# Mamba scan on one core: the product for the state behind the block products, its sum behind y

## The chip, the cores and the metric

The kernel runs on one NeuronCore of one Trainium2 chip. The metric is the device time of one execution in microseconds, lower is better. It is given as the median of several runs.

## The reference

One block of a model: half a feed-forward layer, a Mamba-2 mixer (the "attention" of the names), and half a feed-forward layer again, each behind a layer norm, for 2048 tokens of 256 channels in float32. What the change touches is the mixer's recurrence:

```python
dt = jax.nn.softplus(dt + dt_bias)
A = -jnp.exp(A_log)
dA = jnp.exp(dt * A).reshape(b, l, G, HPG)
dtx = dt.reshape(b, l, G, HPG)[..., None] * x

def step(state, inp):
    dA_t, dtx_t, B_t, C_t = inp
    state = state * dA_t[..., None, None] + jnp.einsum('bgcp,bgn->bgcpn', dtx_t, B_t)
    y_t = jnp.einsum('bgn,bgcpn->bgcp', C_t, state)
    return (state, y_t)
...
y = jnp.moveaxis(ys, 0, 1) + D.reshape(1, 1, G, HPG, 1) * x
...
yn = (yg * lax.rsqrt(var + EPS)).reshape(b, l, INTER) * norm_w
out = yn * jax.nn.silu(z)
return out @ out_proj_w
```

There are 64 heads of 8 channels (512 inner channels) and a state of 128 numbers for each channel.

## The kernel before

The program has three stages that follow each other: the first feed-forward layer (it also builds the weights from a lookup table), the input projection with the convolution, and build_scan, which holds the recurrence, the out projection and the second feed-forward layer. The change is in build_scan, which takes 244 to about 430 us of the span for the recurrence.

**How the scan is tiled.** The 2048 tokens are 16 tiles of 128, and a tile is 4 blocks (NB) of 32 tokens (Q). The recurrence is done blockwise. For a tile, y has three parts: "intra", what the tokens of a block give each other (the block products, L855); "prior", what earlier blocks of the same tile give (L942, from w); and what the state before the tile gives (XB, L935). The state after the tile is the decayed old state (tmp, L1215) plus the product "new" (L947) of B with the fourth of GpSimd's weighted inputs w (L1198); VectorE adds the two (L1151).

**How it is staged.** steps() yields 18 steps c. In step c tile a = c is prepared (transposes, decays, masks), tile b_ = c - 1 gets its products and its state, and tile z = c - 2 gets the gate, its variance and the out projection. Each engine has its own program, written out by hand in the order in which it runs, and engines meet at semaphores: wait(engine, name, value) is left out where the value is zero. There is no scheduler: the order on an engine is the order of the source.

**The decays** of a tile come in 5 units that alternate between two PSUM banks (seg): TensorE sums the logs (segments, L840 for unit 0 and L845 for units 1 to 4), ScalarE takes the exponent in place (L991, for unit 0 into "ends", L995), VectorE multiplies by gs into mmat (masked, L1067). Unit n may be written by TensorE once unit n - 2 was read by VectorE ("m_ok").

**TensorE's order in a step** is: transposes of x (L906), of B and its products (L909 to L913), unit 0, transposes of y of tile z (L922), units 1 and 2, XB from the state (L935), prior (L942), new (L947), unit 3, half of the block products (L855), the out projection (L964, L967) and the row sum (L969), the other half of the block products, unit 4.

**VectorE's order** is: xdt (L1092), yf, u and the two sums of squares (L1100 to L1116), masks 1 and 2, y from XB (L1137), prior times its decay (L1141), their sum (L1146), the state's sum (L1151), mask 3, the residual of tile z (L1157), y plus intra (L1162), mask 4.

**GpSimd's order** is: gs (L1210), tmp (L1215), the low part of u (L1221), w of blocks 0 and 1 (L1198), rstd (L1232), w of blocks 2 and 3. The w of blocks 0 to 2 wait for "prior" of the tile before, the w of block 3 waits for "new":

```python
wait(pool, "prior_ok" if n < NB - 1 else "new_ok", a)
```

The last tile needs no state after it, so it has no "new". ScalarE's copy of BG into bg (L1013) also waits for "new_ok", of the tile before the last one.

Of the kernel before, what the change touches and what calls it, by code (L numbers as in the profile page):

```python
# [23 lines left out]
ALU = mybir.AluOpType  # L24
ACT = mybir.ActivationFunctionType

P = 128
# [21 lines left out]
NB = P // Q  # L49
# [704 lines left out]
def build_scan(nc, T, norm, out):  # L754
# [3 lines left out]
    with ExitStack() as ctx:  # L758
# [10 lines left out]
        w = T["w"]  # L769
        ends = [sb(f"ends_{b}", [P, EW]) for b in range(2)]  # L770
        xdt = [sb(f"xdt_{b}", [P, INTER]) for b in range(2)]
        state = [sb(f"state_{b}", [P, INTER]) for b in range(2)]
        bg = [sb(f"bg_{b}", [P, 2 * P + Q]) for b in range(2)]
        gs = [sb(f"gs_{b}", [P, Q]) for b in range(2)]
        tmp, y, yf, sq, u = (sb(n, [P, INTER]) for n in ("tmp", "y", "yf", "sq", "u"))
# [10 lines left out]
        s = {n: sem("c_" + n) for n in names}  # L786
# [7 lines left out]
        LAST = TILES - 1  # L794
# [3 lines left out]
        def wait(eng, name, value):  # L798
            if value > 0:
                eng.wait_ge(s[name], value)  # L800
# [28 lines left out]
        def _(pe):  # L829
# [72 lines left out]
            for a, b_, z, do_a, do_b, do_z in steps():  # L902
# [27 lines left out]
                if do_b:  # L930
                    wait(pe, "xdt_ok", min(a, TILES - 1) + 1)
                    wait(pe, "state_ok", b_ + 1)
                    for b in range(NB):
                        for g in range(4):
                            ins = pe.matmul(XB[Q * g:Q * g + Q, P * b:P * b + P], cv[:, b_, 5, Q * b:Q * b + Q],  # L935
                                            state[b_ % 2][:, P * g:P * g + P], start=True, stop=True)
                    ins.then_inc(s["from_ok"], 1)
                    wait(pe, "w_ok", NB * (b_ + 1) if b_ < LAST else NB * LAST + NB - 1)
                    wait(pe, "y1_ok", b_)
                    for b in range(1, NB):  # L940
                        for g in range(4):
                            ins = pe.matmul(prior[Q * g:Q * g + Q, P * b:P * b + P],  # L942
                                            bg[b_ % 2][:, P + Q * b:P + Q * b + Q], w[:, b - 1, P * g:P * g + P],
                                            start=True, stop=True)
                    ins.then_inc(s["prior_ok"], 1)
                    if b_ < LAST:
                        pe.matmul(new[:, :], bg[b_ % 2][:, 0:P], w[:, NB - 1, :], start=True, stop=True  # L947
                                  ).then_inc(s["new_ok"], 1)
                    else:
                        wait(pe, "m_ok", (UNITS - 1) * TILES)  # L950
                        norm.pe_transpose(pe, 0)
                if do_a:
# [19 lines left out]
                    hidden(0, 0)  # L972
                if do_b:
                    block_products(b_, HG // 2, HG).then_inc(s["intra_ok"], 1)
                if do_a:
                    segments(a, 4)
            for g in range(GROUPS):
# [83 lines left out]
        def _(dve):  # L1061
# [25 lines left out]
            for a, b_, z, do_a, do_b, do_z in steps():  # L1087
# [56 lines left out]
                if do_b:  # L1144
                    wait(dve, "t1_ok", b_ + 1)
                    dve.tensor_tensor(y[:, P:], prior[:, P:], y[:, P:], ALU.add).then_inc(s["y1_ok"], 1)  # L1146
                if do_b and b_ < LAST:
                    wait(dve, "new_ok", b_ + 1)
                    wait(dve, "tmp_ok", b_ + 1)
                    wait(dve, "from_ok", b_)  # L1150
                    dve.tensor_tensor(state[(b_ + 1) % 2][:, :], new[:, :], tmp[:, :], ALU.add).then_inc(s["state_ok"], 1)  # L1151
                if do_a:
                    masked(a, 3)
                if do_z:
# [4 lines left out]
                if do_b:  # L1159
                    wait(dve, "intra_ok", b_ + 1)  # L1160
                    wait(dve, "y1_ok", b_ + 1)
                    dve.tensor_tensor(y[:, :], intra[:, :, :, :].rearrange("p b h d -> p (b h d)"), y[:, :], ALU.add  # L1162
                                      ).then_inc(s["y_ok"], 1)
                if do_a:
                    masked(a, 4)
                if a == LAST - 1:
# [166 lines left out]
```

## Time and profile before

| | us |
|---|---|
| median of 3 runs | 528.63 |
| lowest and highest run | 528.18 and 531.5 |
| the profiled execution | 529.64 |
| its span | 527.9 |
| TensorE busy in the span | 473.7 (90%) |
| TensorE's weight loads | 396.9 (75%) |
| VectorE busy | 373.4 (71%) |
| ScalarE busy | 285.5 (54%) |
| GpSimd busy | 160.8 (30%) |

The span is what the trace covers, and some 1.7 us of the execution's time lie outside it. In the rows, PE is TensorE's matmuls, PEld its weight loads, DVE is VectorE, ACT is ScalarE and POOL is GpSimd. A matmul that multiplies in float32 stands as two records, so "x64" in the trace is 32 matmuls. The end of a matmul is modelled, so two records that follow each other can overlap by a tenth. A row of the windows view gives the stretch, its length, the busy time of PE, PEld, DVE, ACT and POOL with the number of instructions, the granted TensorE clock as a share of 2.4 GHz, the mean busy share of the DMA engines and the rate. "Issue" is time in which an engine waited for nothing that the trace shows.

### The profile page before, as it was taken

The numbers are of one execution on the slowest core, as the hardware profiler recorded it, in microseconds if no ns is written. First come the engines' busy times: TensorE is split into PE (matmuls) and PEld (weight loads), VectorE is DVE, ScalarE is ACT, GpSimd is POOL, SyncE is SP. The second block draws the span as 40 slices with busy tenths as digits, with TensorE's granted clock in tenths as the row PEclk, the third lists the DMA queues.
The fourth block names the chain that finished last, engine by engine and source line by source line (L and its number), as shares of the span: only waits on it lengthen the run. The fifth ranks groups of instructions, "written<-read, shape, count | busy, mean of one in ns | idle before, by whom it ended". The sixth has DMA issues, their size and how long they took to land.

```text
span 527.9 us, 17119 instructions
## 1 busy us (share of the span) xinstructions
PE 473.7 (90%) x7478; PEld 396.9 (75%) x7478; DVE 373.4 (71%) x736; ACT 285.5 (54%) x515; POOL 160.8 (30%) x216
## 2 busy tenths in 40 slices
PE   4999999999989889366899999999968899999996
PEld 3658797988878668355778877888666778898986
DVE  6998836465659996942688888888758966565543
ACT  3658525252447769796576666566645533233241
POOL 1100040203141221004567766676646411000000
PEclk9999999999999989688899999999999999999999
DMA  8950070000000000010000000000170000101011
GB/s 205 237 197 1 1 338 1 1 1 1 0 1 0 2 0 1 0 40 22 4 6 4 5 4 6 6 4 4 50 297 4 3 3 0 41 1 40 1 40 41
DMA packets 7163, 21.31 MB, mean 40 GB/s; under 512 B 688, under 2 KB 5296, under 8 KB 6448
## 3 DMA queue, kind: packets, MB, share of 16 engines
q1 hardware_dynamic: 6688, 18.05, 10.2%
q10 hardware_dynamic: 400, 2.16, 1.8%
q8 instruction: 59, 0.97, 0.7%
q14 instruction: 16, 0.13, 0.1%
HBM read 12.87 MB, written 6.55 MB: 37 GB/s over the span
## 4 chain that ended last, share of the span: by engine, by line
PE 39%; issue 5%; DVE 3%; ACT 3%; POOL 3%; POOLq 0%; DVEq 0%; ACTq 0%
PE intra L855 6%; PE seg L845 3%; PE yo L964 3%; PE XB L935 2%; PE new L947 1%; PE XB L906 1%; PE seg L840 1%; POOL w L1198 1%; PE yo L922 1%; PE yo L967 1%; PE prior L942 1%; ACT seg L991 1%; DVE mmat L1067 1%; PE XB L68 1%; PE BG L68 1%
## 5 line engine op out<-in xcount | busy, mean ns | idle before, releaser
L1198 POOL TENSOR_TENSOR w<-xdt,ends 32x512 f32<-32x512 f32 (+3 forms) x63 | 66.5, 1074 | 3.1 <-PE prior L942 3.1
L614 DVE SCALAR_TENSOR_TENSOR cv<-pre,vec,cv 128x512 f32<-128x512 f32 x72 | 53.2, 750 | 8.0 <-ACT cv L657 6.3
L991 ACT ACTIVATE seg<-seg 128x512 f32<-128x512 f32 x64 | 36.0, 578 | 32.8 <-PE seg L845 32.5
L1067 DVE TENSOR_TENSOR mmat<-seg,gs 128x512 f32<-128x512 f32 x64 | 42.4, 684 | 10.3 <-ACT seg L991 10.2
L506 POOL TENSOR_TENSOR n_rstd<-n_ve,m_half 128x4 f32<-128x4 f32 x12 | 13.8, 1146 | 115.7 <-DVE n_ve L502 115.7
L845 PEld LDWEIGHTS seg<-abk,m_seg 96*32 96x32 bf16 x2048 | 20.6, 96 | 27.2 <-DVE mmat L1067 14.4
L845 PE MATMUL seg<-abk,m_seg 96*32 96x64 bf16 x2048 | 27.3, 195 | 10.8 <-issue 7.3
L1004 ACT ACTIVATE f_hT<-f_h 128x512 fp32r<-128x512 f32 (+1 forms) x24 | 15.2, 632 | 40.1 <-DVE f_h L1078 40.1
L68 PE MATMUL pj<-n_xT,win 128*128 128x512 f32 x88 | 35.6, 405 | 1.1 <-PEq L130 1.1
L70 PE MATMUL pj<-n_xT,win 128*128 128x512 f32 x88 | 34.8, 395 | 0.0
L69 PE MATMUL pj<-n_xT,win 128*128 128x512 f32 x88 | 34.7, 395 | 0.0
L371 ACT ACTIVATE f_hT<-f_h 128x512 fp32r<-128x512 f32 (+1 forms) x24 | 15.2, 633 | 34.6 <-DVE f_h L295 34.5
L1221 POOL TENSOR_TENSOR uh<-u,uh 128x512 fp32r<-128x512 f32 x16 | 21.0, 1313 | 40.5 <-ACT uh L1025 37.9
L1082 DVE TENSOR_TENSOR f_hT<-f_h,f_hT 128x512 fp32r<-128x512 f32 (+1 forms) x24 | 16.6, 691 | 16.8 <-ACT f_hT L1004 16.8
L299 DVE TENSOR_TENSOR f_hT<-f_h,f_hT 128x512 fp32r<-128x512 f32 (+1 forms) x24 | 16.6, 690 | 14.0 <-ACT f_hT L371 14.0
L255 DVE TENSOR_SCALAR mask_d<-gu_idx,entry 128x1408 fp32r<-128x1408 int32 x28 | 24.4, 947 | 2.3 <-DMA gu_idx<-in_gu 2.3
L367 ACT ACTIVATE f_sg<-f_gate 128x512 f32<-128x512 f32 (+1 forms) x24 | 14.1, 587 | 19.2 <-PE f_gate L70 19.0
L68 PE MATMUL f_down<-wd,f_hT 128*128 128x256 f32 x80 | 22.9, 286 | 0.3 <-ACT wd L344 0.3
L69 PE MATMUL f_down<-wd,f_hT 128*128 128x256 f32 x80 | 22.5, 281 | 0.0
L70 PE MATMUL f_down<-wd,f_hT 128*128 128x256 f32 x80 | 22.5, 281 | 0.0
L295 DVE TENSOR_TENSOR f_h<-f_sg,f_up 128x512 f32<-128x512 f32 x20 | 13.7, 685 | 10.7 <-PE f_up L70 7.4
L68 PEld LDWEIGHTS pj<-n_xT,win 128*128 128x128 f32 x88 | 17.1, 194 | 4.6 <-issue 1.2
(244 smaller groups left out, 1455.2 us busy)
## 6 DMA issues: line engine op xcount, KB each, us to landing
wgu_dram<-wgu SPq DMA_DIRECT2D x1, 2816.0 KB, 8.2
wgu<-wgu_dram SPq DMA_DIRECT2D x1, 2816.0 KB, 10.4
out<-x_res SPq DMA_DIRECT2D x4, 512.0 KB, 2.9
x_res<-in_x SPq DMA_DIRECT2D x1, 1536.0 KB, 23.8
wd_dram<-wd SPq DMA_DIRECT2D x1, 1536.0 KB, 11.6
wd<-wd_dram SPq DMA_DIRECT2D x1, 1536.0 KB, 13.7
gu_idx<-in_gu ACTq DMA_DIRECT2D x4, 352.0 KB, 7.9
gu_idx<-in_gu SPq DMA_DIRECT2D x4, 352.0 KB, 12.5
```

The lines of the kernel that those rows point to most:

```text
L68: pe.matmul(out, w_hi, x_hi, start=start, stop=False)
L69: pe.matmul(out, w_hi, x_lo, start=False, stop=False)
L70: return pe.matmul(out, w_lo, x_hi, start=False, stop=stop)
L255: dve.tensor_scalar(dst, src, entry[:, p:p + 1], None, ALU.is_equal).then_inc(mask_ok, 1)
L299: dve.tensor_tensor(low_part(hT, c, r), h[0:r, :], hT[0:r, 0, c, :].bitcast(F32), ALU.subtract).then_inc(h_lo, 1)
L614: dve.scalar_tensor_tensor(dst, pre[:, x, k:k + GN].rearrange("p (t c) -> p t c", c=P), cw[:, x, k:k + 1], dst, ALU.mult, ALU.add).then_in ...
L845: ins = pe.matmul(out[Q * b:Q * b + Q, i, :], T["m_seg"][:, IU * (n - 1) + i, :], T["abk"][:, b, a, :], start=True, stop=True)
L855: ins = pe.matmul(intra[Q * g:Q * g + Q, :, hh, :], mmat[b_ % 2][:, :, h], xbd[b_ % 2][:, h, :, :], start=True, stop=True)
L991: act.activation(seg[u_ % 2][:, :, :], seg[u_ % 2][:, :, :], ACT.Exp).then_inc(s["exp_ok"], 1)
L1067: dve.tensor_tensor(mmat[a % 2][:, i, :], seg[u_ % 2][:, :, :], gs[a % 2][:, i].unsqueeze(2).broadcast_to([P, IU, HEADS]), ALU.mult).then_ ...
L1198: pool.tensor_tensor(heads(w[r, n, :]), heads(xdt[a % 2][r, :]), ends[a % 2][r, n * HEADS:(n + 1) * HEADS].unsqueeze(2) .broadcast_to([Q * ...
L1221: pool.tensor_tensor(uh[:, 1, :, :].rearrange("p g t -> p (g t)"), u[:, :], uh[:, 0, :, :].bitcast(F32).rearrange("p g t -> p (g t)"), ALU ...
```

## The change

TensorE issues "new" no longer behind prior but behind the second half of the block products, ahead of unit 4; there it waits for all four w of the tile. At the old place the wait for w is one less, since prior reads only three of them. VectorE adds the state no longer behind the sum of y and prior but behind the sum of y and intra, ahead of mask 4. The waits of GpSimd and ScalarE read as before.

```diff
--- before.py
+++ after.py
@@ -935,7 +935,7 @@
                             ins = pe.matmul(XB[Q * g:Q * g + Q, P * b:P * b + P], cv[:, b_, 5, Q * b:Q * b + Q],
                                             state[b_ % 2][:, P * g:P * g + P], start=True, stop=True)
                     ins.then_inc(s["from_ok"], 1)
-                    wait(pe, "w_ok", NB * (b_ + 1) if b_ < LAST else NB * LAST + NB - 1)
+                    wait(pe, "w_ok", NB * b_ + NB - 1)
                     wait(pe, "y1_ok", b_)
                     for b in range(1, NB):
                         for g in range(4):
@@ -943,10 +943,7 @@
                                             bg[b_ % 2][:, P + Q * b:P + Q * b + Q], w[:, b - 1, P * g:P * g + P],
                                             start=True, stop=True)
                     ins.then_inc(s["prior_ok"], 1)
-                    if b_ < LAST:
-                        pe.matmul(new[:, :], bg[b_ % 2][:, 0:P], w[:, NB - 1, :], start=True, stop=True
-                                  ).then_inc(s["new_ok"], 1)
-                    else:
+                    if b_ == LAST:
                         wait(pe, "m_ok", (UNITS - 1) * TILES)
                         norm.pe_transpose(pe, 0)
                 if do_a:
@@ -972,6 +969,11 @@
                     hidden(0, 0)
                 if do_b:
                     block_products(b_, HG // 2, HG).then_inc(s["intra_ok"], 1)
+                if do_b and b_ < LAST:
+                    wait(pe, "w_ok", NB * (b_ + 1))
+                    wait(pe, "state_ok", b_ + 1)
+                    pe.matmul(new[:, :], bg[b_ % 2][:, 0:P], w[:, NB - 1, :], start=True, stop=True
+                              ).then_inc(s["new_ok"], 1)
                 if do_a:
                     segments(a, 4)
             for g in range(GROUPS):
@@ -1144,11 +1146,6 @@
                 if do_b:
                     wait(dve, "t1_ok", b_ + 1)
                     dve.tensor_tensor(y[:, P:], prior[:, P:], y[:, P:], ALU.add).then_inc(s["y1_ok"], 1)
-                if do_b and b_ < LAST:
-                    wait(dve, "new_ok", b_ + 1)
-                    wait(dve, "tmp_ok", b_ + 1)
-                    wait(dve, "from_ok", b_)
-                    dve.tensor_tensor(state[(b_ + 1) % 2][:, :], new[:, :], tmp[:, :], ALU.add).then_inc(s["state_ok"], 1)
                 if do_a:
                     masked(a, 3)
                 if do_z:
@@ -1161,6 +1158,11 @@
                     wait(dve, "y1_ok", b_ + 1)
                     dve.tensor_tensor(y[:, :], intra[:, :, :, :].rearrange("p b h d -> p (b h d)"), y[:, :], ALU.add
                                       ).then_inc(s["y_ok"], 1)
+                if do_b and b_ < LAST:
+                    wait(dve, "new_ok", b_ + 1)
+                    wait(dve, "tmp_ok", b_ + 1)
+                    wait(dve, "from_ok", b_)
+                    dve.tensor_tensor(state[(b_ + 1) % 2][:, :], new[:, :], tmp[:, :], ALU.add).then_inc(s["state_ok"], 1)
                 if do_a:
                     masked(a, 4)
                 if a == LAST - 1:
```

**TensorE, one step in the middle of the scan.** A row is a line of the source, its operation, the tile that it writes, the tiles that it reads, and its shape. Before:

```order
L942 MATMUL prior<-w,bg 32x128 x12
L947 MATMUL new<-w,bg 128x512
L845 MATMUL seg<-abk,m_seg 32x64 x32
L855 MATMUL intra<-xbd_even,mmat 32x4x8 x32
L964 MATMUL yo<-wout,uh 128x256 x8
L967 MATMUL yo<-wout,uh 128x256 x4
L969 MATMUL yo<-ones,ssum 128x1
L855 MATMUL intra<-xbd_even,mmat 32x4x8 x32
L845 MATMUL seg<-abk,m_seg 32x64 x32
L906 MATMUL XB<-ident,cv 128x128 x4
```

After (the lines from L947 on have moved up by three, so that L961, L964 and L966 are L964, L967 and L969 of before):

```order
L942 MATMUL prior<-w,bg 32x128 x12
L845 MATMUL seg<-abk,m_seg 32x64 x32
L855 MATMUL intra<-xbd_even,mmat 32x4x8 x32
L961 MATMUL yo<-wout,uh 128x256 x8
L964 MATMUL yo<-wout,uh 128x256 x4
L966 MATMUL yo<-ones,ssum 128x1
L855 MATMUL intra<-xbd_even,mmat 32x4x8 x32
L975 MATMUL new<-w,bg 128x512
L845 MATMUL seg<-abk,m_seg 32x64 x32
L906 MATMUL XB<-ident,cv 128x128 x4
```

The product "new" has moved behind unit 3, both halves of the block products and the out projection, and stands directly in front of unit 4, behind which the next step's transposes begin.

**VectorE, the same stretch,** from the masks of units 1 and 2 to the next step's xdt. Before:

```order
L1067 TENSOR_TENSOR mmat<-seg,gs 128x512 x2
L1137 TENSOR_TENSOR y<-XB,dl 128x512
L1141 TENSOR_TENSOR prior<-prior,dl 128x384
L1146 TENSOR_TENSOR y<-prior,y 128x384
L1151 TENSOR_TENSOR state<-new,tmp 128x512
L1067 TENSOR_TENSOR mmat<-seg,gs 128x512
L1157 SCALAR_TENSOR_TENSOR x_res<-yo,rstd_y,x_res 128x256
L1162 TENSOR_TENSOR y<-intra,y 128x512
L1067 TENSOR_TENSOR mmat<-seg,gs 128x512
L1092 TENSOR_TENSOR xdt<-XB,dt_tok 128x512
L1100 SCALAR_TENSOR_TENSOR yf<-cv,vec,yo 128x128 x4
```

After (lines are two further down, L1165 is the state's sum):

```order
L1069 TENSOR_TENSOR mmat<-seg,gs 128x512 x2
L1139 TENSOR_TENSOR y<-XB,dl 128x512
L1143 TENSOR_TENSOR prior<-prior,dl 128x384
L1148 TENSOR_TENSOR y<-prior,y 128x384
L1069 TENSOR_TENSOR mmat<-seg,gs 128x512
L1154 SCALAR_TENSOR_TENSOR x_res<-yo,rstd_y,x_res 128x256
L1159 TENSOR_TENSOR y<-intra,y 128x512
L1165 TENSOR_TENSOR state<-new,tmp 128x512
L1069 TENSOR_TENSOR mmat<-seg,gs 128x512
L1094 TENSOR_TENSOR xdt<-XB,dt_tok 128x512
L1102 SCALAR_TENSOR_TENSOR yf<-cv,vec,yo 128x128 x4
```

The sum of the state has moved behind mask 3, the residual and the sum of y, and stands in front of mask 4 and of the next step's xdt.

## Rows read from the trace of the kernel before

**Rows 1.** Waits of the scan, 244 to 415 us: total us, times, longest us

```profile
PEld seg L845 <- DVE mmat L1067: 14.4, 16, 1.6
```

**Rows 2.** Timeline, one step: start us, us, engine line op out<-in xcount [idle before <-releaser]

```profile
343.97 2.11 POOL L1198 TENSOR_TENSOR w<-xdt,ends 96x512 f32<-96x512 f32 x2
...
344.36 0.66 PE L906 MATMUL XB<-ident,cv 128*128 128x128 f32 x4
...
345.13 0.69 DVE L1067 TENSOR_TENSOR mmat<-seg,gs 128x512 f32<-128x512 f32 x1
...
345.62 0.41 ACT L1013 ACTIVATE bg<-BG 128x288 f32<-128x288 f32 x1 [0.52 <-PE BG L913]
...
346.60 1.12 DVE L1100 SCALAR_TENSOR_TENSOR yf<-cv,vec,yo 128x128 f32<-128x128 f32 x4 [0.18 <-PE yo L922]
...
348.87 1.12 PE L947 MATMUL new<-w,bg 128*128 128x512 f32 x2
...
349.30 1.28 DVE L1067 TENSOR_TENSOR mmat<-seg,gs 128x512 f32<-128x512 f32 x2
...
350.04 0.42 PE L845 MATMUL seg<-abk,m_seg 96*32 96x64 bf16 x32
...
350.28 1.15 PE L855 MATMUL intra<-xbd,mmat 128*32 128x32 f32 x64
...
351.36 1.22 PE L964 MATMUL yo<-wout,uh 128*128 128x256 f32 x8
...
352.16 0.68 DVE L1151 TENSOR_TENSOR state<-new,tmp 128x512 f32<-128x512 f32 x1
...
353.09 1.14 PE L855 MATMUL intra<-xbd,mmat 128*32 128x32 f32 x64
...
354.04 0.46 PE L845 MATMUL seg<-abk,m_seg 96*32 96x64 bf16 x32
...
354.43 0.66 PE L906 MATMUL XB<-ident,cv 128*128 128x128 f32 x4
```

**Rows 3.** Timeline, the same place in two other steps

```profile
328.01 1.13 PE L947 MATMUL new<-w,bg 128*128 128x512 f32 x2
...
328.24 1.28 DVE L1067 TENSOR_TENSOR mmat<-seg,gs 128x512 f32<-128x512 f32 x2
...
329.06 0.42 PE L845 MATMUL seg<-abk,m_seg 96*32 96x64 bf16 x32
...
382.11 1.28 DVE L1067 TENSOR_TENSOR mmat<-seg,gs 128x512 f32<-128x512 f32 x2
...
382.85 0.42 PE L845 MATMUL seg<-abk,m_seg 96*32 96x64 bf16 x32
```

**Rows 4.** Windows, 12 steps (length, busy times, PEclk, DMA share, GB/s), and timeline, one hole

```profile
271.02:402.38 131.36, 122.77 (x4352) 102.89 (x4345) 107.01 (x218) 80.77 (x156) 88.01 (x97) 1.00 0.10 39
...
390.54 0.41 PE L845 MATMUL seg<-abk,m_seg 96*32 96x64 bf16 x31 [2.63 <-issue]
```

**Rows 5.** Timeline, step 15 and the start of step 16

```profile
410.07 0.42 PE L845 MATMUL seg<-abk,m_seg 96*32 96x64 bf16 x32 [0.74 <-DVE mmat L1067]
...
415.35 0.66 PE L922 MATMUL yo<-ident,y 128*128 128x128 f32 x4 [0.82 <-DVE y L1162]
```

**Rows 6.** Windows: four stretches of the scan, columns as in rows 4

```profile
245.00:255.00 10.00, 6.95 (x284) 5.74 (x280) 5.15 (x8) 9.03 (x17) 5.79 (x8) 0.88 0.01 3
...
344.36:354.43 10.07, 10.02 (x369) 8.36 (x363) 8.86 (x19) 6.70 (x13) 7.31 (x9) 1.00 0.02 5
384.00:392.00 8.00, 5.19 (x174) 4.80 (x174) 3.66 (x7) 1.71 (x4) 4.01 (x5) 1.00 0.98 419
406.00:412.00 6.00, 4.72 (x159) 3.66 (x160) 5.90 (x13) 3.85 (x8) 4.71 (x6) 1.00 0.01 4
```

**Rows 7.** DMA queues of the page: packets, MB, share of 16 engines

```profile
q8 instruction: 59, 0.97, 0.7%
```

**Rows 8.** Line L935: duration ns min/median/max, first and last start us

```profile
L935 PE MATMUL XB<-state,cv x512: 269/273/421, 252.2 to 416.7; 128*32 128x128 f32 x171
```


## The prediction

> **What bounds the kernel now.** I read the waits over the scan first, then one step of it in the timeline, then the same place in two other steps, then the busy times over 12 steps, and last the stretches that are not like the others.
>
> The waits show that TensorE is the engine the scan waits on, with one regular exception: the segment matmuls wait for VectorE's masks, 14.4 us in 16 times on the weight loads [rows 1]. In that view no TensorE line waits for GpSimd's w (L1198): the wait on "w_ok" that the change loosens costs nothing today.
>
> One step tells where the exception sits [rows 2]. I count from its first transpose, L906 at 344.36; the next is at 354.43, so a step is 10.07 us. The segment matmul of unit 3 starts at 350.04, 5.68 us in. The first half up to there is a chain: transposes of y, then yf on VectorE at 346.60 (which waited 0.18 for them), the square on ScalarE, the sums and the first mask at 349.30. One mask takes 0.69 (345.13), so it ends at 349.99, and TensorE goes on 0.05 us after it. TensorE's own work there (up to prior) ends near 348.87, where "new" starts. So "new" lies in a hole of about 1.1 us that TensorE has anyway. The second half, 350.04 to 354.43, is 4.39 us of TensorE work end to end: segments, half of the block products, the out projection (L964), the other half at 353.09, segments at 354.04, transposes.
>
> Does "new" or the mask open unit 3? In two other steps [rows 3] the mask ends at 382.11 + 0.69 = 382.80 with segments at 382.85 (0.05 behind it, as above), and at 328.24 + 0.69 = 328.93 with segments at 329.06. Only the second is later than 0.05, by 0.08; there "new", started at 328.01, is what ended last, and it held TensorE 1.05 us. So mask and "new" end together almost to a tenth: the matmul fills the hole exactly.
>
> Twelve steps in a row, from the L906 at 271.02 to that at 402.38, take 131.36 us [rows 4]; 12 times 10.07 is 120.84. The other 10.5 us are holes that the trace calls "issue"; the longest, 2.63 us, stands in front of segments at 390.54 [rows 4].
>
> **The change part by part.**
>
> *The matmul leaves the first half.* TensorE then waits for the mask from the end of prior on. The chain over yf, square and mask has no step that waits for "new", so its 5.68 us stay. Gain: the excess of 0.08 us in a few steps, 0.2 us in all. Bounds: 0, or 14 times 1.05 if the mask were not the gate.
>
> *It comes back behind the second half of the block products.* No hole is there, so it is paid in full. Its body is 1.05 us [rows 3]. Its edges cost too: from the first of a half's block products to what follows takes 350.28 to 351.36, 1.08 us, where a full-width matmul follows, and 353.09 to 354.04, 0.95 us, where segments follow [rows 2]. So 0.13 more for changing to a 128-row matmul, 1.18 us a step. From below I bound it by 1.05, if the edge costs nothing, from above by 1.12 (its modelled length at 348.87) plus twice the edge, 1.38. I take 1.18, since the rows for body and edge are its own.
>
> There are 15 such products, 14 of them in steps that have an out projection. In the first one (step 1) TensorE has no hole at the old place, so the move costs only the edge, 0.13. Thirteen steps pay 1.18: 15.3 us. The fifteenth (step 15, where unit 3 waits 0.74 us for the mask because VectorE first takes the layer-norm statistics) is followed by y's transposes that wait 0.82 us for VectorE [rows 5]. That wait hides part of the matmul, but the state's sum (0.68 us) now stands before mask 4 and the normalisation, which TensorE's next transposes need. I count 1.0, bounds 0.3 and 1.3.
>
> *VectorE: the sum moves behind y, before mask 4.* It waits for "new", which ends where the segments of unit 4 begin, 0.39 us before the next step (354.04 against 354.43). So it runs from about -0.33 to +0.35 of the next step. Behind it stand mask 4, xdt and yf. Mask 4 starts at +0.77 (345.13) because ScalarE's exponent of unit 4 comes only then; that is what hides the sum, with 0.4 us to spare. y itself ends before, as its block products end 1.4 us before the step. Cost nothing; 0.68 a step if that cover is gone. Mask 3 comes 0.68 earlier, which nobody waits for.
>
> *The waits on w and state.* "prior" now needs three of the four w instead of four: worth nothing [rows 1]. GpSimd's fourth w (one of two in 2.11 us, 343.97) now waits for "new" of the same step: it runs from -0.39 to +0.68. Queued behind it is gs, which cannot start before ScalarE's copy of BG (345.62 + 0.41, that is +1.67), then tmp. So it has 1.0 us of room; without it, masks would be late by up to 1.07 a step. The state is there at +0.35 and wanted later: by tmp, which stands behind gs, and by XB, which stands behind y's transposes (yf starts on their end, 346.60, at +2.24). No DMA is issued or passed.
>
> *Issue holes.* They total 10.5 us. The same instructions now run in steps 1.1 us longer, and TensorE waits 1.1 us near the middle, in which whatever feeds it can catch up; a hole ahead of yf still lengthens the chain. Bounds: all 10.5 gone, or 2 more through another alignment. I take 2.0 off, because the largest ones stand at 384 to 392, where transfers are 98% busy [rows 6], and will stay.
>
> Sum: 15.3 + 1.0 + 0.1 - 0.2 - 2.0 = 14.2 us. The profiled execution took 529.64 us (span 527.9, 1.7 around it), so 543.8. The median of the runs shown is 528.63, 1.0 less; I predict 543.0.
>
> **Rivals.**
>
> *The loading of TensorE's code paces the holes* (chance 0.11). There are 59 loads of 0.97 MB together, 16.4 KB each [rows 7]. The Trainium skill, page "Advanced Engine Details and Errata", section "ISA Cache", says that instructions come in blocks of 16 KB, 256 instructions; the rows agree. If the added wait cures all 10.5 us: 16.2 - 10.5 = +5.7, 534.3. For it: holes sit in front of the densest instruction runs. Against: the step of [rows 2] has 10.02 us busy in 10.07 at the same density [rows 6], and the longest hole comes with the transfers.
>
> *"new" was the gate* (0.06): then 1.05 leaves the first half and only the edges stay, 14 x 0.13 = 1.8, minus the holes: 529. For it: in all three steps read the segments begin about when "new" ends. Against: segments 0.05 us behind the mask in two of the three steps read.
>
> *Faster: code loading is the bound of the whole scan* (0.03). Then the matmul's time at its new place, in front of the segments where the 2.63 hole stands, is spent loading, and the holes go as well: 528.6 - 10.5 = 518. It decides from where a step without holes would still take longer than its matmuls. Against: the same row, TensorE 10.02 us busy in 10.07 [rows 6].
>
> *VectorE or GpSimd late into the next step* (0.06): if the state's sum does not fit in front of mask 4, 14 x 0.68 = 9.5 more, 552.
>
> *TensorE's clock falls* (0.04). It stood at 0.88 in 245 to 255 with TensorE 6.95 of 10 us busy, so part of that was at 1.2 GHz, and at 1.00 in 406 to 412 with 4.72 of 6 busy; a new step has 10.0 of 11.2 busy [rows 6]. An XB matmul takes 421 ns at most against 273 in the median [rows 8]. One step in four at that ratio: 3.5 x 10 x 0.54 = 19 us more on top of the forecast, 562. The Trainium skill, page "TensorE: Matmul & The Clock Gate", section "A second HAM failure mode: psum-queue depth-cycling", says that frequent short pauses between groups of matmuls make the clock swing between its levels. By that rule a pause in every step is bad; the row of 406 to 412, with pauses of 0.7 and more, does not bear it out.
>
> **How the numbers follow.** The forecast has 0.70. Its own range is 538 to 547 (price 1.05 to 1.38 a step, holes by -5 to +2, not all at their ends together); the range of 8 in 10 reaches down to the code-loading case: 535 to 547. A measurement of this kernel tells about 1% from no change, that is 523.3 to 533.9. Faster by over 1%: 0.03. Within 1%: 0.06 of "new was the gate" and 0.04 of the low edge of the code-loading case, 0.10. Slower: 0.87.
>
> **What would show it.** In the profile after, a step without holes lasts 11.25 us; its unit-3 segments start 5.7 us in and wait about 1.1 us for the mask, so the waits of segments for masks go from 14.4 to about 28 us on the weight loads; "new" stands between the block products and the segments, 1.2 us from the one to the other; mask 4 still starts 0.8 us into the step, and gs at 1.7. I am wrong if the first half shrinks to about 4.6 us, if yf starts behind xdt instead of the transposes, or if issue holes in the scan fall by more than 5 us.

## The result and the profile after

The changed kernel takes 539.61 us (median of 4 runs, 538.27 to 541.06) against 530.03 us of the kernel before (median of 4, 528.18 to 531.5): ratio 1.0183, 95% interval 1.0132 to 1.0235. It is slower, by 9.6 us. The profiled execution took 541.06 us, the slowest of the four, against 529.64 us before: 11.4 us more in the two traces.

The page of the changed kernel begins:

```profile
span 539.3 us, 17134 instructions
...
PE 473.0 (88%) x7478; PEld 395.9 (73%) x7478; DVE 375.4 (70%) x736; ACT 285.0 (53%) x515; POOL 161.2 (30%) x216
...
PEclk9999999999999989679999999999979999999999
...
q8 instruction: 59, 0.97, 0.7%
```

The busy times are those of before to 2 us; what is new is idle time of TensorE. The waits of the changed kernel from 244 to 430 us (total us, times, longest us) say in front of what:

```profile
PEld seg L845 <- DVE mmat L1069: 22.4, 16, 2.1
...
PE seg L845 <- DVE mmat L1069: 18.4, 16, 1.8
...
POOL w L1200 <- PE new L975: 10.6, 14, 5.1
...
DVE state L1165 <- PE new L975: 2.0, 3, 1.3
```

The first line answers to [rows 1]: the weight loads waited 14.4 us for masks before. The matmul line of before was:

```profile
PE seg L845 <- DVE mmat L1067: 2.8, 8, 0.9
```

So TensorE itself now waits 15.6 us more for masks, 1.1 us in each of 14 steps. GpSimd's fourth w waits for "new", as its place in the new order says.

One step of the changed kernel in the timeline, which answers to [rows 2]:

```profile
338.69 0.69 DVE L1165 TENSOR_TENSOR state<-new,tmp 128x512 f32<-128x512 f32 x1
...
338.83 1.08 POOL L1200 TENSOR_TENSOR w<-xdt,ends 128x512 f32<-128x512 f32 x1 [0.33 <-PE new L975]
...
338.93 0.66 PE L906 MATMUL XB<-ident,cv 128*128 128x128 f32 x4
...
339.70 0.69 DVE L1069 TENSOR_TENSOR mmat<-seg,gs 128x512 f32<-128x512 f32 x1 [0.31 <-ACT seg L993]
...
340.67 0.25 POOL L1212 TENSOR_TENSOR gs<-bg,tri 128x32 f32<-128x32 f32 x1 [0.77 <-ACT bg L1015]
...
341.17 1.12 DVE L1102 SCALAR_TENSOR_TENSOR yf<-cv,vec,yo 128x128 f32<-128x128 f32 x4 [0.19 <-PE yo L922]
...
343.87 1.28 DVE L1069 TENSOR_TENSOR mmat<-seg,gs 128x512 f32<-128x512 f32 x2
...
344.61 0.42 PE L845 MATMUL seg<-abk,m_seg 96*32 96x64 bf16 x32 [1.23 <-DVE mmat L1069]
...
347.67 1.14 PE L855 MATMUL intra<-xbd_even,mmat 128*32 128x32 f32 x64
...
348.74 1.13 PE L975 MATMUL new<-w,bg 128*128 128x512 f32 x2
...
349.80 0.42 PE L845 MATMUL seg<-abk,m_seg 96*32 96x64 bf16 x32
...
350.15 0.66 PE L906 MATMUL XB<-ident,cv 128*128 128x128 f32 x4
```

The reader is to see four things. Unit 3 starts at +5.68 of the step, to the hundredth where it was, and TensorE has waited 1.23 us for it. The step is 11.22 us long instead of 10.07. From the block products to "new" are 1.07 us and from there to the segments 1.06, 2.13 together, where 0.95 stood before: 1.18 more. And both covers hold: mask 4 starts at +0.77, gs at +1.74, yf behind the transposes at +2.24.

Ten steps (3 to 12) and then two (13 and 14, in which the last part's weights are loaded), first of the kernel before, then of the changed one (length, busy time of PE, PEld, DVE, ACT and POOL, clock, DMA share, GB/s):

```profile
271.02:376.63 105.61, 101.94 (x3628) 85.55 (x3621) 88.91 (x181) 67.19 (x130) 73.50 (x81) 1.00 0.02 5
376.63:402.38 25.75, 20.83 (x728) 17.34 (x725) 18.10 (x38) 13.58 (x26) 14.52 (x17) 1.00 0.45 178
```

```profile
271.53:383.85 112.32, 100.12 (x3632) 84.94 (x3621) 90.22 (x181) 67.03 (x130) 73.41 (x81) 1.00 0.02 5
383.85:412.66 28.81, 22.83 (x735) 18.74 (x725) 18.13 (x37) 13.41 (x26) 14.69 (x17) 0.88 0.40 158
```

The ten steps grew by 6.7 us, not by ten times 1.13 = 11.3. Before, they held 4.9 us above ten times 10.07, the step of [rows 2], in which TensorE is not held up; below, what a trace's steps take above such a step of the same kernel is called its holes. Now the steps average 11.23 and hold next to nothing above 11.2. So 4.6 us of holes are gone there. That is what the experiments had to explain. The other parts of the 11.4 us: steps 1 and 2 +0.5, steps 13 and 14 +3.1, everything behind them +1.1.

### The profile page after: what moved, and what is told of

Same layout as the page of the kernel before. It is cut to its first block, busy times and chain, and to the rows that moved or that the text cites. A ratio compares the mean times of both kernels' runs of the same rounds, so it can differ in the third digit from the quotient of the medians.

```text
span 539.3 us, 17134 instructions
## 1 busy us (share of the span) xinstructions
PE 473.0 (88%) x7478; PEld 395.9 (73%) x7478; DVE 375.4 (70%) x736; ACT 285.0 (53%) x515; POOL 161.2 (30%) x216
## 4 chain that ended last, share of the span: by engine, by line
PE 38%; issue 5%; DVE 5%; ACT 4%; POOL 2%; DVEq 0%; POOLq 0%; ACTq 0%
PE intra L855 6%; PE seg L845 3%; PE new L975 3%; PE yo L961 3%; DVE mmat L1069 2%; ACT seg L993 2%; ACT sq L1024 2%; PE XB L906 2%; PE seg L840 1%; PE yo L964 1%; PE yo L922 1%; DVE ssum L1115 1%; PE XB L68 1%; PE BG L68 1%; PE intra L68 1%
## 5 line engine op out<-in xcount | busy, mean ns | idle before, releaser
L1069 DVE TENSOR_TENSOR mmat<-seg,gs 128x512 f32<-128x512 f32 x64 | 42.4, 685 | 11.2 <-ACT seg L993 11.1
L845 PEld LDWEIGHTS seg<-abk,m_seg 96*32 96x32 bf16 x2048 | 19.1, 96 | 38.8 <-DVE mmat L1069 22.4
L845 PE MATMUL seg<-abk,m_seg 96*32 96x64 bf16 x2048 | 25.3, 196 | 19.8 <-DVE mmat L1069 18.4
L855 PE MATMUL intra<-xbd_even,mmat 128*32 128x32 f32 x1024 | 18.8, 224 | 4.3 <-issue 4.3
L1154 DVE SCALAR_TENSOR_TENSOR x_res<-yo,rstd_y,x_res 128x256 f32<-128x256 f32 x16 | 7.7, 483 | 20.0 <-POOL rstd_y L1234 20.0
```

Of the source, the lines that this page charges most:

```text
L845: ins = pe.matmul(out[Q * b:Q * b + Q, i, :], T["m_seg"][:, IU * (n - 1) + i, :], T["abk"][:, b, a, :], start=True, stop=True)
L855: ins = pe.matmul(intra[Q * g:Q * g + Q, :, hh, :], mmat[b_ % 2][:, :, h], xbd[b_ % 2][:, h, :, :], start=True, stop=True)
L1069: dve.tensor_tensor(mmat[a % 2][:, i, :], seg[u_ % 2][:, :, :], gs[a % 2][:, i].unsqueeze(2).broadcast_to([P, IU, HEADS]), ALU.mult).then_ ...
```

## The experiments

Each time stands against runs of the kernel before on the same chip; the median of before was 530.21, 530.82 and 530.09 us in the three groups. From each trace I read the length of steps 3 to 12 (start of L906 to start of L906), its mean, and the shortest step. These columns are of one execution each, while the executions of one kernel lie up to 7 us apart, so a difference of 1 or 2 us between two rows of them proves little. In steps 13 and 14 the granted clock differs too: it is 1.00 in before, e3, e7, e10 and e11, 0.88 in the changed kernel, and 0.82 to 0.94 in the others. In steps 3 to 12 it is 1.00 everywhere but in e8 (0.92).

| run | us | ratio, 95% interval | steps 3 to 12, us | mean step | shortest | steps 13 and 14 |
|---|---|---|---|---|---|---|
| before (profiled run) | 529.64 | | 105.61 | 10.56 | 10.04 | 25.75 |
| changed (profiled run) | 541.06 | 1.0183 (1.0132 to 1.0235) | 112.32 | 11.23 | 11.17 | 28.81 |
| e1_sum_only | 531.18 | 1.002 (0.9995 to 1.0046) | 105.07 | 10.51 | 10.13 | 27.66 |
| e2_behind_unit3 | 540.23 | 1.019 (1.0144 to 1.0235) | 112.30 | 11.23 | 11.20 | 27.22 |
| e3_fill_hole | 533.68 | 1.0061 (1.003 to 1.0092) | 107.94 | 10.79 | 10.21 | 26.58 |
| e4_narrow_old | 528.82 | 0.9983 (0.9953 to 1.0012) | 104.55 | 10.46 | 10.04 | 25.84 |
| e5_narrow_new | 532.62 | 1.0029 (0.9997 to 1.0061) | 110.53 | 11.05 | 10.45 | 26.37 |
| e6_shift_before | 534.39 | 1.0058 (1.0033 to 1.0084) | 107.78 | 10.78 | 10.06 | 25.86 |
| e7_split_load | 527.05 | 0.9904 (0.9862 to 0.9946) | 105.84 | 10.58 | 10.05 | 22.46 |
| e8_more_code | 580.64 | 1.0917 (1.0868 to 1.0966) | 143.03 | 14.30 | 12.15 | 31.88 |
| e9_less_code | 521.58 | 0.9834 (0.9806 to 0.9861) | 100.86 | 10.09 | 10.05 | 24.79 |
| e10_split12 | 533.73 | 1.0058 (1.0032 to 1.0084) | 106.09 | 10.61 | 10.06 | 26.03 |
| e11_after_split | 534.58 | 1.0083 (1.0054 to 1.0113) | 112.16 | 11.22 | 11.18 | 22.38 |

**e1_sum_only.** One half of the change alone, in the kernel before: VectorE's sum for the state goes behind y, and "new" stays where it was.

```diff
@@ vector
-                if do_b and b_ < LAST:
-                    wait(dve, "new_ok", b_ + 1)
...
-                    dve.tensor_tensor(state[(b_ + 1) % 2][:, :], new[:, :], tmp[:, :], ALU.add).then_inc(s["state_ok"], 1)
                 if do_a:
                     masked(a, 3)
...
                                        ).then_inc(s["y_ok"], 1)
+                if do_b and b_ < LAST:
+                    wait(dve, "new_ok", b_ + 1)
...
+                    dve.tensor_tensor(state[(b_ + 1) % 2][:, :], new[:, :], tmp[:, :], ALU.add).then_inc(s["state_ok"], 1)
                 if do_a:
                     masked(a, 4)
```

> Only VectorE's sum of the state moves (behind y, ahead of mask 4); "new" stays behind prior on TensorE. My theory: the sum cost nothing in the changed kernel only because "new" delayed the next step's start. Here y runs from +0.15 to +0.83 of the step, the sum to +1.5, mask 4 to +2.2, xdt to +2.9, so yf starts about 0.6 us later than at +2.24 and the first half grows from 5.68 to about 6.3 us: 14 x 0.6 = 8 us, less 2 to 5 us of issue holes that the waits absorb: 533 to 537. Rival (the sum is free at this place in any case): a step of 10.07 us, 530.

Measured: 531.18 us, ratio 1.002, no difference that the interval shows. The shortest step is 10.13 us, 0.1 longer, not 0.6. In its timeline (one step, from the L906 at 290.83):

```profile
291.60 0.68 DVE L1163 TENSOR_TENSOR state<-new,tmp 128x512 f32<-128x512 f32 x1
...
292.19 0.68 DVE L1067 TENSOR_TENSOR mmat<-seg,gs 128x512 f32<-128x512 f32 x1
...
293.39 1.11 DVE L1100 SCALAR_TENSOR_TENSOR yf<-cv,vec,yo 128x128 f32<-128x128 f32 x4
...
294.54 0.63 ACT L1022 ACTIVATE sq<-yf 128x512 f32<-128x512 f32 x1
```

yf does start later, at +2.56 instead of +2.24, but only 0.3 us: VectorE's instructions start 0.60 apart when they queue, not 0.68. And the square stands at +3.71 against +3.6 (347.96 in the step of [rows 2]), since ScalarE is busy with its exponents until then and hides the rest. The 0.6 us that I expected here were six times too many; the order of VectorE is not where the time goes.

**e2_behind_unit3.** TensorE's product alone, at another place in the second half.

```diff
@@ tensor, from the kernel before
-                    wait(pe, "w_ok", NB * (b_ + 1) if b_ < LAST else NB * LAST + NB - 1)
+                    wait(pe, "w_ok", NB * b_ + NB - 1)
...
-                    if b_ < LAST:
-                        pe.matmul(new[:, :], bg[b_ % 2][:, 0:P], w[:, NB - 1, :], start=True, stop=True
...
-                    else:
+                    if b_ == LAST:
...
                     segments(a, 3)
+                if do_b and b_ < LAST:
+                    wait(pe, "w_ok", NB * (b_ + 1))
+                    pe.matmul(new[:, :], bg[b_ % 2][:, 0:P], w[:, NB - 1, :], start=True, stop=True
+                              ).then_inc(s["new_ok"], 1)
```

> Only TensorE's product moves, to right behind the segments of unit 3; the sum stays behind y1 on VectorE. My theory: the price is paid for leaving the hole ahead of unit 3, wherever in the second half it lands: steps without holes of 11.15 to 11.25 us, issue holes small outside the weight load, 539 to 541. Rival (the place directly ahead of unit 4 is what removes the issue holes, or the late sum is part of the price): holes of 4 to 5 us come back, 543 to 545, or steps shorter than 11.1.

Measured: 540.23 us, ratio 1.019, and the ten steps take 112.30 us, the changed kernel's 112.32 again. Its timeline, the segments of unit 3 first:

```profile
333.12 0.42 PE L845 MATMUL seg<-abk,m_seg 96*32 96x64 bf16 x32 [0.74 <-DVE mmat L1068]
333.47 1.13 PE L953 MATMUL new<-w,bg 128*128 128x512 f32 x2
334.52 1.13 PE L855 MATMUL intra<-xbd,mmat 128*32 128x32 f32 x64
```

So the whole loss is that the product left the hole. Neither these two places in the second half nor the place of the sum make a difference.

**e3_fill_hole.** The changed kernel with other work in the hole.

```diff
@@ tensor, from the changed kernel
-                if do_a:
-                    segments(a, 3)
                 if do_b:
...
                     block_products(b_, 0, HG // 2)
+                if do_a:
+                    segments(a, 3)
```

> The changed kernel, with the first half of the block products (1.08 us) put into the emptied hole, ahead of unit 3. My theory: the hole takes any 1.1 us of work, so the first half stays near 5.7 and the second falls from 5.53 to about 4.5: steps of 10.1 to 10.25. If the issue holes were cured by TensorE's wait, they come back: 530 to 533. If they were cured by the other order alone they stay away: 526 to 528.

Measured: 533.68 us, ratio 1.0061. The shortest step is 10.21 us, as forecast: 1.0 of the 1.13 us come back once something of that length stands in front of the mask. The issue holes came back as well (107.94 us, 5.8 above ten times 10.21), more than I expected, and the run lies just above the 530 to 533 forecast for that case. The other order alone did not remove them.

**e4_narrow_old.** The kernel before, "new" cut to 16 columns: the other 496 of the state's update aren't computed (VectorE clears the bank once ahead of the scan).

```diff
@@ tensor, from the kernel before
-                        pe.matmul(new[:, :], bg[b_ % 2][:, 0:P], w[:, NB - 1, :], start=True, stop=True
+                        pe.matmul(new[:, 0:16], bg[b_ % 2][:, 0:P], w[:, NB - 1, 0:16], start=True, stop=True
```

> The kernel before, with "new" cut to 16 of its 512 columns at its old place (the state's update is left out for the other heads), so that TensorE waits about 0.9 us there in every step. My theory: the mask, not "new", opens unit 3, so a step without holes stays at 10.0 to 10.07 us; and if a wait of TensorE cures the issue holes, 4 to 5 us go: 525 to 526. Rivals: "new" was the gate: steps of 9.2 us, 515 to 518; the wait cures nothing: 529 to 530.

Measured: 528.82 us, ratio 0.9983, its interval across 1. One step's rows:

```profile
283.64 0.39 PE L947 MATMUL new<-w,bg 128*128 128x16 f32 x2
...
284.19 1.28 DVE L1067 TENSOR_TENSOR mmat<-seg,gs 128x512 f32<-128x512 f32 x2
...
284.93 0.42 PE L845 MATMUL seg<-abk,m_seg 96*32 96x64 bf16 x32 [0.90 <-DVE mmat L1067]
```

This step takes 10.06 us from L906 to L906 (the shortest 10.04), with TensorE idle for 0.90 of it. The rival that "new" opened unit 3 has fallen: it was free where it stood. And my idea that a wait of TensorE cures the holes has fallen too: the ten steps still hold 4.1 us of them. A wait that does not lengthen the step changed nothing here.

**e5_narrow_new.** The same cut in the changed kernel (the edit of e4_narrow_old at the new place).

> The changed kernel with "new" cut to 16 of its 512 columns (the state's update is left out for the other heads). Splits the price of a step, 1.13 us in the changed kernel's hole-free steps (11.2 against 10.07), into body and edge. My theory: the body is the 512 columns streamed, some 0.85 us of it goes, and the edges around a full-width matmul of about 0.3 stay: hole-free steps of 10.35 us. At that step the code loading is again close to its pace, so some issue holes return: 530 to 533. Rival (the price is not the columns but the switch of shape): steps of 11.0 or more.

Measured: 532.62 us, shortest step 10.45 us. In its timeline, with block products, "new" and the segments of unit 4:

```profile
288.23 1.14 PE L855 MATMUL intra<-xbd,mmat 128*32 128x32 f32 x64
...
289.30 0.40 PE L975 MATMUL new<-w,bg 128*128 128x16 f32 x2
...
289.62 0.42 PE L845 MATMUL seg<-abk,m_seg 96*32 96x64 bf16 x32
```

1.07 us to "new" (against 0.95 to the segments before, the edge of 0.12) and 0.32 from there on, where the full one takes 1.06. So of 1.18 us about 0.74 is the streaming of 496 columns and 0.44 is a fixed price of a full-width matmul at that place. The holes were larger than before (6.0 us above ten times 10.45), which I had not expected of a longer step.

**e6_shift_before.** The kernel before, its code shifted.

```diff
@@ tensor, ahead of the loop over steps
+            for _ in range(32):
+                pe.transpose(yo[:, 0:P], T["ident"][:, :], T["ident"][:, :])
```

> The kernel before with 32 more transposes (64 records and their weight loads) ahead of the scan, into a bank that is free then, so that the blocks of TensorE's code fall a half block elsewhere in the steps. Pace theory: code is loaded at one block per about 3.7 us at best, a step holds 2.8 blocks, so the holes sit at other places and their sum over the scan stays at 4 to 6 us outside the weight load: 530 to 533 with about 1 to 2 us for the transposes themselves. Rival (the holes come from an unlucky alignment): they go, 526 or less, or double.

Measured: 534.39 us, ratio 1.0058, above the 530 to 533 forecast. The 32 transposes account for most of it: the first step starts at 246.32 us instead of 243.46. The ten steps of the trace take 107.78 us, 2.2 more than before, but it is of the slowest of the nine executions (537.48 us), so what the shift does to the sum of the holes is not shown to a microsecond or two. The holes stand at other steps, and do not vanish: an unlucky alignment does not make them.

**e8_more_code.** The changed kernel with more instructions in TensorE's wait.

```diff
@@ tensor, ahead of segments(a, 3), from the changed kernel
+                if do_a and do_b and b_ < LAST:
+                    for i in range(96):
+                        pe.matmul(BG[Q * (i % NB):Q * (i % NB) + Q, 320:384], T["m_seg"][:, i % Q, :],
+                                  T["abk"][:, i % NB, a, :], start=True, stop=True)
```

> The changed kernel with 96 small matmuls more in each step's hole ahead of unit 3 (about 1 us of TensorE time there, written to columns that nobody reads). They fit into the 1.1 us that TensorE waits, so by TensorE's time alone a step stays at 11.2 us and the run at 540 to 541. Pace theory: they add 192 instructions to about 724, a step then holds 3.6 blocks instead of 2.8, at 3.7 us a block that is 13.2 us a step: 14 x 2.0 = 28 us more, 565 to 570.

Measured: 580.64 us, ratio 1.0917. It is worse than the pace theory said, and nowhere near what TensorE's time says (540 to 541). Its code loads on the page, and two holes from its timeline:

```profile
q8 instruction: 70, 1.15, 0.9%
```

```profile
310.64 0.79 PE L951 MATMUL BG<-abk,m_seg 96*32 96x64 bf16 x76 [0.67 <-issue]
311.23 0.46 PE L845 MATMUL seg<-abk,m_seg 96*32 96x64 bf16 x32
311.57 0.54 PE L855 MATMUL intra<-xbd_even,mmat 128*32 128x32 f32 x20
314.48 0.91 PE L855 MATMUL intra<-xbd_even,mmat 128*32 128x32 f32 x44 [2.37 <-issue]
```

Between the two holes stand 76 + 32 + 20 = 128 matmul records, each with its weight load: 256 instructions. The change adds 15 x 192 = 2880 instructions, and the page 11 loads to the 59: some 260 instructions a load. Ten steps hold 4581 weight loads and 4592 matmuls here, 917 records a step, against 725 before. In blocks of 256 that is 3.58 and 2.83. The mean step divided by that is 4.0 us a block here; before it is 10.56 / 2.83 = 3.73. Part of the 4.0 is not loading: the granted clock over these ten steps is 0.92, so TensorE stood at 1.2 GHz for about a sixth of them.

**e9_less_code.** The kernel before with fewer instructions. It leaves out half of the products XB from the state (two of four blocks) and two of the three blocks of prior, 16 matmuls a step (64 records: each float32 matmul stands as two, each with its weight load). VectorE clears the bank of prior once ahead of the scan.

```diff
@@ tensor
-                    for b in range(NB):
+                    for b in range(2):
                         for g in range(4):
                             ins = pe.matmul(XB[Q * g:Q * g + Q, P * b:P * b + P], cv[:, b_, 5, Q * b:Q * b + Q],
...
-                    for b in range(1, NB):
+                    for b in range(1, 2):
```

> The kernel before with half of the XB products and two thirds of the prior products left out (y lacks parts of the state's and the earlier blocks' shares): 64 instructions less per step, all ahead of unit 3, where TensorE then waits longer for the same mask. A step without holes stays at 10.07 us by the mask and the second half, and holds 2.6 blocks of code instead of 2.8; at 3.7 us a block that is 9.6 us, less than the step. Pace theory: the holes outside the weight load go, 4 to 6 us: 525 to 527, steps of 10.05 to 10.15. e4_narrow_old, which kept the number of instructions and kept its holes, is the other half of this comparison. Rival (holes have nothing to do with the amount of code): 530.

Measured: 521.58 us, ratio 0.9834, some 4 us below the forecast of 525 to 527. Of the 9.2 us between this trace and that of before, 4.8 lie in the ten steps, 2.0 in steps 1 and 2, 1.0 in steps 13 and 14, and 1.5 ahead of the scan, where the two programs are alike. Ten steps and the two behind them:

```profile
267.44:368.30 100.86, 91.21 (x3307) 75.92 (x3301) 88.66 (x181) 67.06 (x130) 73.10 (x81) 1.00 0.02 5
368.30:393.09 24.79, 20.82 (x667) 17.04 (x661) 17.81 (x37) 13.49 (x26) 14.62 (x17) 0.86 0.47 184
```

The step stays at 10.05 us by mask and second half, and the holes of the ten steps are all but gone: 100.86 us, one wait of 0.3 us left. Beside e4_narrow_old (less TensorE time, same number of instructions, TensorE idle for 0.9 us a step as it is here, holes kept) this shows that the number of instructions per microsecond makes the holes, not how busy TensorE is.

**Where the holes stand.** The traces kept settle what a hole is. I count TensorE's records in each trace, weight loads, matmuls and semaphore instructions together, and look at every wait of TensorE over 0.25 us that is named "issue" in steps 1 to 14. There are 121 of them in the 13 traces, and each stands at record 193, 194 or 195 of a row of 256. In e6_shift_before, which has 128 records more ahead of the scan, they stand at the same numbers, and so at other places of the step. Each wait ends 1.2 to 1.7 us after a transfer of queue q8 has ended, the queue that loads code. So a hole is TensorE at the end of a block of code, waiting for the next one.

The same records show why it comes late: in steps 3 to 12 of before, the load of a block starts 1.1 us (median) after TensorE has entered the block ahead of it, takes 0.9 to 1.4 us, and TensorE goes on 1.2 to 1.6 us later. Together that was 3.55 to 4.06 us a block in front of the seven waits of those steps, against the 3.56 us in which a step of 10.07 us uses a block up.

**e7_split_load, e10_split12 and e11_after_split.** The load of the last part's weights in pieces, in the kernel before (six and twelve) and in the changed one (six). Each piece is waited for before the next is issued; the diff is that of six, behind which TensorE waits for 96 instead of 32. Twelve halve each of these pieces once more.

```diff
@@ sync, from the kernel before
-            for name in ("wgu", "wd"):
-                sp.dma_start(chip, T[name + "_dram"]).then_inc(loaded, 16)
-            sp.wait_ge(loaded, 32)
+            pieces = [("wgu", h, k) for h in range(2) for k in range(KC)] + [("wd", h, None) for h in range(2)]
+            for n, (name, h, k) in enumerate(pieces):
+                at = (slice(None), h, k) if k is not None else (slice(None), h)
+                sp.dma_start(T[name][at].bitcast(F32), T[name + "_dram"][at]).then_inc(loaded, 16)
+                sp.wait_ge(loaded, 16 * (n + 1))
```

> The kernel before with the load of the last part's weights (4.3 MB in two transfers at 380 us) cut into six transfers, each waited for before the next. The long issue holes of 2.6 us and more stand inside that load. If the loads of TensorE's code queue behind the transfers, the pauses let them through and 2 to 3 us go: 527 to 528. If not, or if the pieces only spread the same holes over a longer stretch: 530.

> As e7_split_load (six transfers, ratio 0.990) with twelve transfers, each waited for before the next. If what matters is that the code loads find a pause, finer pieces may gain another 1 us: 526; if the load then ends too late for the last part (12 pieces of 3 us from 380 on are 416 us, it is wanted at about 421), a wait appears there: 528 or more.

> The changed kernel with the load in six transfers. If the long hole of 3.5 us at 393 and the late step behind it are the code loads behind the transfers, 4 to 5 us go: 535 to 536, and the price of the change against e7_split_load (527) is then 8 to 9 us. If the hole in the changed kernel is of another kind: 539 to 540.

Measured: six pieces give 527.05 us, ratio 0.9904, faster than both kernels. Steps 13 and 14 go from 25.75 to 22.46 us:

```profile
376.72:399.18 22.46, 20.68 (x726) 17.31 (x725) 18.10 (x38) 13.58 (x26) 14.53 (x17) 1.00 0.47 140
```

The longest issue hole there is now 1.09 us. What the whole load does to the code is in the trace of before: the block behind the 2.63 us hole was loaded in 0.94 us, but its load started 4.1 us after TensorE had entered the block ahead of it, instead of the usual 1.1; in the changed kernel's 3.52 us hole it was 4.9 us. In these two holes the code load started late behind the transfers; it did not run slower. Twelve pieces give it back (533.73): its trace shows holes of 0.92 and 1.66 us in these steps and a load that still issues transfers behind 411 us. The late end that I had allowed for is there: TensorE waits 1.38 us for the second weight (wd) at 425.38, and what lies behind step 14 takes 2.1 us longer than before. That the holes return too is not explained. In the changed kernel six pieces give 534.58 us, steps 13 and 14 take 22.38 us, two times 11.19, and the long hole is gone. Against e7_split_load it is 7.5 us slower, by medians of two groups, or 8.3 when each is first set against the kernel before in its own group.

## Why the prediction was right, and what was off

The measured 539.61 us lies in the range of 535 to 547, and the sign was right; the forecast of 543.0 was 3.4 us high.

*What bounds the kernel, and the first half.* Right. Unit 3 stays at +5.68 us, e4_narrow_old shows that "new" was free at its old place, and e2_behind_unit3 that leaving it costs all.

*The price of 1.18 us a step.* 1.18 was measured between block products and segments. The whole step grew by 1.13 to 1.15, as the segments to the transposes take 0.04 us less. Over 13 steps that is some 0.5 us of my excess.

*VectorE, GpSimd, the waits.* Right: mask 4 at +0.77, gs at +1.74, no wait behind them. GpSimd's fourth w runs later than I placed it, from -0.10 to +0.98 instead of -0.39 to +0.68, which still leaves 0.77 us of its room. The price named for a lost cover, 0.68 us a step, was wrong: e1_sum_only paid 0.1. The waits on the weight loads went to 22.4 us, not to about 28: they had waited 0.9 us each already (14.4 us in 16 times), and now wait 1.50 us in front of unit 3.

*Step 15 and behind.* 1.0 us counted, 1.1 measured.

*Issue holes.* This is the term that was mis-sized: I took 2.0 us off for the whole scan, since the large ones stand in the weight load, and the runs show about 5.8. Between the two traces, steps 3 to 12 lost 4.6 us, nearly all that they had. Steps 13 and 14 stood 5.6 us above two steps without holes and now stand 6.4 above, but 2.5 of these are a slow clock (below), so their holes fell by 1.7. Steps 1 and 2 gained 0.5, their waits named "issue" going from 1.6 to 2.1. By this account a sign that I had named for being wrong, holes that fall by more than 5 us, came true, though the time is in the range. The reason that I gave, a wait in which the loader catches up, is wrong for e4_narrow_old; what the runs show in its place is the mechanism of the rival "the loading of TensorE's code paces the holes", though not its 10.5 us: a block of code comes late when the blocks are used up faster than one in 3.6 to 4 us, and fewer instructions per microsecond, by a longer step (changed kernel, e2_behind_unit3, e11_after_split) or by less code (e9_less_code), let it come in time.

*The sum.* The traces differ by 11.4 us: 16.0 for the prices as measured, 5.8 less for holes, 1.2 more for the clock, which I had at nothing. That the forecast of 14.2 missed by only 2.8 is in part luck, since the clock gave back a third of what the holes were mis-sized by.

*The base.* I started from a median of 528.63 us of three runs. With the fourth it is 530.03, and in the three later groups 530.1 to 530.8. The profiled execution, at 529.64, was the better base; the correction by 1.0 us was worth nothing.

*The clock.* The rival put the fall into every step, which was wrong, but the clock did fall once. Timeline and windows of the changed kernel behind its long hole:

```profile
397.20 0.33 PE L855 MATMUL intra<-xbd_even,mmat 128*32 128x32 f32 x3 [3.52 <-issue]
397.45 2.08 PE L975 MATMUL new<-w,bg 128*128 128x512 f32 x2
```

```profile
338.93:350.15 11.22, 9.99 (x375) 8.49 (x363) 9.03 (x19) 6.70 (x13) 7.35 (x9) 1.00 0.02 4
...
397.00:403.00 6.00, 5.80 (x68) 3.85 (x68) 2.67 (x4) 1.01 (x3) 1.49 (x3) 0.50 0.41 171
```

With 1.2 us of wait in every step the granted clock stays at 1.00 through ten of them; behind one idle stretch of 3.52 us it stands at half, 1.2 GHz, for 6 us, and "new" takes 2.08 instead of 1.13 us. Set against the same matmuls of the step at 338.93, this stretch costs 2.5 us. The kernel before has its slow stretch elsewhere, in step 1: granted clock 0.86 over the step, TensorE busy 9.47 us, against 1.00 and 8.12 us in the changed kernel, with 355 matmul records in both. So some 1.3 us come back there (my estimate from these two rows), which is also why steps 1 and 2 grew by 0.5 us and not by the 1.3 that their prices say. The Trainium skill ("TensorE: Matmul & The Clock Gate", "A second HAM failure mode: psum-queue depth-cycling") warns of frequent short pauses; this trace does not show that for pauses of 1.2 us. The trace of e8_more_code agrees better: with its code waits of up to 2.4 us the granted clock goes to half seven times in ten steps. The idle stretch alone does not decide it, as it stays at 1.00 behind the 2.63 us of the kernel before.

**What stays open.** Before, a block of code comes every 3.73 us on average, in e4_narrow_old every 3.69, but e3_fill_hole, e6_shift_before and e5_narrow_new hold holes at 3.81, 3.81 and 3.90 us. So there is no single pace. One part that moves is the code load itself: its median in steps 3 to 12 is 0.98 us in before, 1.01 in e4, 1.12 in e3, 1.21 in e6 and 1.23 in e5. Why it differs is not known. Nor is what TensorE does in the 1.2 to 1.7 us between the end of a load and its next instruction.

## What to carry to other kernels

Before a matmul is moved, look at what stands in front of the next wait: if the wait ends a chain on other engines, the work in front of it is free as long as it fits, and where TensorE works end to end it is paid in full with its edges. A trace's "issue" holes on TensorE can be a matter of instructions per microsecond: count the records between two of them, and if they are multiples of 256, it is the code. A change that lengthens the step can make them vanish, and one that shortens it can bring them back, so the gain or loss of a step is partly given back. A large transfer during dense small matmuls may be worth cutting into a few pieces that wait for each other; here six gained 1.0% and twelve lost it again.

## What the runs showed of the hardware

Some 725 TensorE records a step at 10.07 us (2.83 blocks of 256, 3.56 us each) are more than the code loads sustained here; 661 are not. The code loads on the page are 59 for the kernel, 70 with 96 matmuls more in 15 steps, and 55 in e9_less_code:

```profile
q8 instruction: 55, 0.90, 0.7%
```

The 64 records a step that e9_less_code leaves out are, over 16 steps, 4 blocks of 256, and 4 loads fewer are counted. That agrees with the block of 256 instructions that the Trainium skill states ("Advanced Engine Details and Errata", "ISA Cache"), and so do the places of the holes. Two things I had not expected. TensorE's code is loaded only one block ahead here: the load starts about 1.1 us after the block in front of it was entered, and a dense stretch of small matmuls uses a block up in 3.56 us. And 4.3 MB in two transfers cost 3.3 us of two steps against the same bytes in six, by the late start of code loads; with six, the two steps of the changed kernel take 22.38 us, two times 11.19.
